# Causal attention on one core: value and output tables multiplied once, probabilities applied tile by tile, expert weights loaded behind the first key move

## The chip, the cores and the metric

One core of a Trainium2 chip runs a chain of eight layers (four attention-like, four feed-forward) on 4096 tokens of 128 features, all in one program. The metric is the device time of one launch in microseconds (us). Five engines run side by side, each in its own program order, and wait for each other by semaphores: TensorE (PE), VectorE (DVE), ScalarE (ACT), GpSimd (POOL) and SyncE (SP), which here issues the DMAs. PE's weight loads stand in a row of their own, PEld.

## The reference: what the touched stage computes

Only the third pair of layers is touched: causal attention with one head of 64 features, then a choice of one expert of eight per token. `x` is the residual stream, 8 chunks of 512 tokens; S and E of this layer are 512 and 128 here.

```python
q, k, v = x @ wq + bq, x @ wk + bk, x @ wv + bv          # 128 -> 64 each
w = softmax(q k^T / 8 + causal mask)                     # 512 x 512 per chunk
z = (w @ v) @ wo + bo                                    # 64 -> 128
# then, on the layer-normalised sum:
idx = argmax(xf @ Wg + bg)                               # one of 8 experts
h = gelu(xf @ W1[e] + b1[e])                             # all 8 are computed, 128 -> 128
y = h @ W2[e] + b2[e];  out = y[idx]
```

## The kernel before

`causal_and_gelu` (line 1815) builds the stage out of one instruction list per engine; nothing reorders them. A chunk c is 512 tokens, four tiles of 128. The loop `for s in steps` runs s from -2 to 8, and in one step the experts of chunk s stand between the second half of attention of chunk s+1 and the first half of chunk s+2. All matmuls are float32, which PE does in two passes (so the trace has two records for one matmul; a transpose is one).

One step on PE, in this order: `weigh(s+1)` (probabilities times values), `up(s, 0)` and `up(s, 1)` (two experts' first layer, each 512 tokens), `project(s+1)` (output table), `turn_first(s+2)` (transposes of the normalised tokens), `up` 2 and 3, `queries_and_keys(s+2)`, `values(s+2)`, `up` 4 to 7, `scores(s+2)`, then the four pieces of `down(s)` with `turn_second(s+1)`, `logits(s+1)`, `turn_prob(s+2)` and `turn_choice(s+1)` between them. `up(e)` waits for the gelu two before it, since there are two PSUM banks for it.

ACT in one step: `copy_weighed(s+1)` (z from PSUM to SBUF), gelu 0 and 1, `copy_first(s+2)`, gelu 2 and 3, `copy_queries_and_keys`, `copy_values`, gelu 4 to 7, `root(s+1)`, `exponentials(s+2)`, `copy_choice(s+1)`. A change of function table is an instruction of its own, ACT_TABLE_LOAD, placed ahead of the first operation that needs it: there are three in a step (gelu, square root, exponential).

DVE in one step: `add_output(s-1)` and its statistics, `keep_chosen(s, 1)` (expert 1's rows masked), `add_attention(s+1)` (scaled output added to x), `keep_chosen(s, 3)`, statistics, `normal_first(s+3)`, `keep_chosen` 5, 6, 7, `maxima(s+2)`, `normal_second(s+1)`, `copy_second`, `choose`, `copy_prob(s+2)`. POOL does `keep_chosen` 0, 2, 4 and `add_bias`.

SP issues, in order: the loads of the small tables, W1, b1, W2 and b2 of the experts (W1 and W2 are 512 KB each), and then per step `move_keys(st+2)` (the keys from partitions 64..127 of `qk` to `kT`, without which `scores` cannot start) and `spread_choice(st+1)` (the chosen rows to DRAM, and four loads that spread them over all partitions into `G`, which every `keep_chosen` needs).

The PSUM bank `ups` is shared in turn by the values, z, the projected output, the bias row, the logits and the choice. `bc` is the bias row (bv @ wo + bo); it waits for `copy_values(0)`.

Of the kernel before, what the change touches and what calls it, by code (L numbers as in the profile page):

```python
# [12 lines left out]
B, S, D = 8, 512, 128  # L13
# [1801 lines left out]
def causal_and_gelu(nc, net, d):  # L1815
# [8 lines left out]
    with ExitStack() as ctx:  # L1824
# [9 lines left out]
        xn1, xc, qk, kT, V = two("xn1", [TC, D]), two("xc", [S]), two("qk", [S]), two("kT", [S], H), two("V", [TC, H])  # L1834
        nb, sums, ri, prob = two("nb", [TC]), two("sums", [TC]), two("ri", [TC]), two("prob", [10 * P])
        PT, zT = [two(f"PT{k}", [(TC - k) * P]) for k in range(TC)], two("zT", [S], H)
# [19 lines left out]
        s_ready, nb_done, p_done, p_turned, PT_done, z_ready, z_done, o_ready = (  # L1856
            p.sem(n) for n in ("s_ready", "nb_done", "p_done", "p_turned", "PT_done", "z_ready", "z_done", "o_ready"))
# [23 lines left out]
        def _(sp):  # L1881
# [14 lines left out]

            sp.dma_start(wqk[:, 0:H], a("wq")).then_inc(qk_loaded, 16)
# [9 lines left out]
            sp.dma_start(W1[:, :, :], d["L2_ffn_W1"].rearrange("e d f -> d e f")).then_inc(e_loaded, 16)  # L1907
            sp.dma_start(b1[:, :], d["L2_ffn_b1"]).then_inc(e_loaded, 16)
            sp.dma_start(W2[:, :, :], d["L2_ffn_W2"].rearrange("e f d -> f e d")).then_inc(e_loaded, 16)
            sp.wait_ge(rest_zeroed, 1)  # L1910
            sp.dma_start(b2[0:E, :], d["L2_ffn_b2"]).then_inc(e_loaded, 16)
# [41 lines left out]
        def _(pe):  # L1953
# [36 lines left out]
            def weigh(c):  # L1990
                pe.wait_ge(PT_done, c + 1)
                pe.wait_ge(v_done, c + 1)
                wait_for(pe, ohT_done, c - 1)
                for k in range(TC):
                    last = nc.tensor.matmul(ups[0:H, k * P:S], V[c % 2][:, k, :], PT[k][c % 2][:, :],
                                            start=(k == 0), stop=(k == TC - 1))
                last.then_inc(z_ready, 1)

            def project(c):
                pe.wait_ge(z_done, c + 1)  # L2000
                for k in range(TC):
                    last = nc.tensor.matmul(ups[:, tok(k)], zT[c % 2][:, tok(k)], wo[:, :], start=True, stop=True)
# [42 lines left out]
            for s in steps:  # L2045
# [9 lines left out]
                if here(s + 1):  # L2055
                    project(s + 1)
# [16 lines left out]
                if here(s + 2) and s + 1 != 0:  # L2073
# [29 lines left out]
        def _(act):  # L2103
            def copy_weighed(c):
                act.wait_ge(z_ready, c + 1)
                wait_for(act, o_ready, c - 2)
                nc.scalar.activation(zT[c % 2][:, :], ups[0:H, :], ACT.Copy).then_inc(z_done, 1)
# [20 lines left out]
            def copy_values(c):  # L2128
                act.wait_ge(v_ready, c + 1)
                wait_for(act, z_ready, c - 2)  # L2130
                nc.scalar.activation(V[c % 2][:, :, :].rearrange("p a b -> p (a b)"), ups[:, 0:TC * H],
# [1034 lines left out]
```

## Time and profile before

| | us |
|---|---|
| median of 3 runs (lowest, highest) | 1577.16 (1574.89, 1578.33) |
| the profiled execution: its own time | 1576.58 |
| its span, first to last instruction | 1574.8 |
| the touched stage in that span | 1056.0 to 1331.7 |
| PE, DVE, ACT, POOL busy over the span | 1288.2, 1029.2, 802.3, 535.9 |
| granted TensorE clock over the span | 0.885 of full speed |

The touched stage is a sixth of the span. Two kinds of stretch stand in it: a start of some 60 us, in which the first two chunks go through attention with little beside them, and eight steps of about 28 us. Busy shares over the whole span say little about it; the places of the stage have to be read in the timeline.

### The profile page before, as it was taken

To read this page: it belongs to the slowest core of one execution; us is meant where nothing else is said; L and a number is where in the kernel's file an instruction comes from. 1 tells how busy PE (TensorE), PEld (TensorE's weight loads), DVE (VectorE), ACT (ScalarE), POOL (GpSimd) and SP (SyncE) were. 2 spreads that over 40 slices of the span, in tenths; PEclk is the share of its full clock that TensorE was granted. 3 is DMA by queue.
4 is the path that set the end of the run, shared out by engine and by line. 5 is a ranking of instruction groups with operands and counts; after the bars stand their busy time and mean duration, and the time that the engine had idled before them with its cause. 6 is when DMAs were issued, how large, how long until landed. Compare 5 with 4: busy or idle time off the path is not lost. (4 is left out here: it accounts for less than half of the span.)

```text
span 1574.8 us, 21830 instructions
## 1 busy us (share of the span) xinstructions
PE 1288.2 (82%) x6696; PEld 718.4 (46%) x6696; DVE 1029.2 (65%) x2781; ACT 802.3 (51%) x1606; POOL 535.9 (34%) x668
## 2 busy tenths in 40 slices
PE   5899999999997128935589989875899997689898
PEld 1223333333333118932345555643466755577633
DVE  7778888888853665635987785323467653566486
ACT  2467777776783004527646543312455452456554
POOL 3342343343210006358455345330112112333046
PEclk7799999999998558975699999985799998699999
DMA  5211111111105302210023333321132131000001
GB/s 151 57 49 30 52 48 41 42 52 52 32 12 157 70 1 66 59 36 24 8 55 70 72 76 55 76 39 34 58 112 62 62 107 57 30 2 1 1 21 34
DMA packets 80774, 81.15 MB, mean 52 GB/s; under 512 B 19899, under 2 KB 64139, under 8 KB 80659
## 3 DMA queue, kind: packets, MB, share of 16 engines
q1 hardware_dynamic: 77327, 74.06, 18.0%
q0 software_dynamic: 2304, 4.72, 1.3%
q8 instruction: 54, 0.88, 0.2%
q10 hardware_dynamic: 1028, 0.98, 0.2%
q14 instruction: 61, 0.50, 0.1%
HBM read 64.32 MB, written 13.92 MB: 50 GB/s over the span
## 5 line engine op out<-in xcount | busy, mean ns | idle before, releaser
L933 DVE TENSOR_REDUCE a_nm<-a_aps 128x1 f32<-128x512 f32 x512 | 333.5, 686 | 75.2 <-PE a_aps L698 75.2
L897 ACT ACTIVATE a_prob<-a_sps 128x512 f32<-128x512 f32 x512 | 271.4, 597 | 114.6 <-PE a_sps L710 113.6
L698 PE MATMUL a_aps<-a_K,a_Q 96*128 96x512 bf16 x512 | 195.1, 401 | 13.0 <-DMA a_K<-k_parts 12.7
L710 PE MATMUL a_sps<-a_Q,a_K 99*128 99x512 bf16 x512 | 156.2, 385 | 1.2 <-ACT a_prob L897 1.2
L1402 POOL TENSOR_TENSOR p_h<-p_sl,p_t 128x512 f32<-128x512 f32 x72 | 105.5, 1484 | 143.3 <-ACT p_sl L1542 74.3
L719 PE MATMUL a_ops<-a_prob,a_Vg 128*32 128x512 f32 x1024 | 136.9, 609 | 0.0
L698 PEld LDWEIGHTS a_aps<-a_K,a_Q 96*128 96x128 bf16 x512 | 50.3, 98 | 140.7 <-DVE a_nm L933 90.4
L1542 ACT ACTIVATE p_sl<-p_up_a 128x512 f32<-128x512 f32 x72 | 42.9, 597 | 112.5 <-PE p_up_b L1432 112.5
L1928 POOL TENSOR_TENSOR c_h<-c_h,c_G 128x512 f32<-128x512 f32 x24 | 31.7, 1325 | 181.0 <-ACT c_h L2114 163.8
L407 POOL CAST a_ms<-a_mr 16x128 bf16<-16x128 f32 x32 | 9.0, 280 | 243.0 <-ACT a_mr L855 243.0
L1432 PE MATMUL p_up_b<-x_normT,p1w_w 128*128 128x512 f32 x144 | 76.4, 613 | 7.9 <-DVE p_t L1650 7.6
L1650 DVE TENSOR_TENSOR p_t<-p_G,p_up_b 128x512 f32<-128x512 f32 x64 | 43.8, 685 | 53.5 <-PE p_up_b L1432 33.2
L710 PEld LDWEIGHTS a_sps<-a_Q,a_K 99*128 99x128 bf16 x512 | 49.8, 99 | 61.1 <-ACT a_prob L897 30.5
L1430 PE MATMUL p_up_a<-x_normT,p1w_w 128*128 128x512 f32 x144 | 74.8, 601 | 1.5 <-ACT p_sl L1542 1.5
L1440 PE MATMUL p_yps<-p1w_w,p_h 128*128 128x128 f32 x576 | 68.6, 282 | 3.2 <-POOL p_h L1402 3.2
L1440 PEld LDWEIGHTS p_yps<-p1w_w,p_h 128*128 128x128 f32 x576 | 67.9, 199 | 4.4 <-issue 3.2
L1204 ACT ACTIVATE m0e_hT<-m0e_hps,m0e_ws 128x128 f32<-128x128 f32 x160 | 45.6, 368 | 41.3 <-PE m0e_hps L1173 41.3
L2041 PE MATMUL c_yps<-c_W,c_h 128*128 128x128 f32 x512 | 64.0, 279 | 0.0
L2275 DVE TENSOR_TENSOR c_h<-c_h,c_G 128x512 f32<-128x512 f32 x40 | 39.9, 1017 | 35.8 <-ACT c_h L2114 32.5
L2031 PE MATMUL c_hps<-c_xT,c_W 128*128 128x512 f32 x128 | 61.9, 613 | 0.0
L2041 PEld LDWEIGHTS c_yps<-c_W,c_h 128*128 128x128 f32 x512 | 61.3, 196 | 0.0
L1155 POOL DMA_INDIRECT m0e_x<-tokens,m0w_token x40 | 39.7, 992 | 49.5 <-PE m0e_xps L1166 23.4
(571 smaller groups left out, 2702.2 us busy)
## 6 DMA issues: line engine op xcount, KB each, us to landing
p_G<-gates_by_expert SPq DMA_DIRECT2D x32, 512.0 KB, 6.9
c_G<-choice_rows SPq DMA_DIRECT2D x32, 512.0 KB, 6.4
a_Q<-q_parts SPq DMA_DIRECT2D x192, 32.0 KB
a_K<-k_parts SPq DMA_DIRECT2D x31, 96.0 KB
q_parts<-a_partsq SPq DMA_DIRECT2D x7, 384.0 KB, 2.8
k_parts<-a_partsk SPq DMA_DIRECT2D x7, 384.0 KB, 2.8
token_outputs<-m0e_y SPq DMA_DIRECT2D x40, 64.0 KB, 1.5
m0w_w<-in_L_ffn_W SPq DMA_DIRECT2D x1, 2048.0 KB, 9.4
```

The lines of the kernel that those rows point to most:

```text
L698: nc.tensor.matmul(aps[n % 3][:, :], Q[0:MAX, head, q * P:(q + 1) * P], K[0:MAX, head, :], start=True, stop=True).then_inc(a_ready, 1)
L710: nc.tensor.matmul(sps[(NS * u + k) % 3][:, :], K[0:KB, head, k % TC * P:(k % TC + 1) * P], Q[0:KB, head, :], start=True, stop=True).then_ ...
L719: last = nc.tensor.matmul(ops[32 * j:32 * j + 32, :], Vg[u % 2][:, k, j, :], prob[u % 2][:, j, k, :], start=(k == 0), stop=(k == TC - 1))
L897: nc.scalar.activation(prob[u % 2][:, k // TC, k % TC, :], sps[n % 3][:, :], ACT.Exp).then_inc(p_done, 1)
L933: nc.vector.tensor_reduce(nm[u % 2][:, s:s + 1], aps[n % 3][:, :], AX.X, ALU.max, negate=True).then_inc(a_used, 1)
L1204: nc.scalar.activation(hT[t % 2][:, f, :], hps[t % 2][:, f * P:(f + 1) * P], ACT.Relu, bias=ws[t % 3][:, B1 + f:B1 + f + 1]).then_inc(h_do ...
L1402: nc.gpsimd.tensor_tensor(h[c % 2][:, j, :], sl[u % 3][:, :], t[u % 3][:, :], ALU.mult).then_inc(h_done, 1)
L1430: nc.tensor.matmul(up_a[u % 2][:, :], w1[:, j, :], net.xT[:, c * S:(c + 1) * S], start=True, stop=True)
L1432: nc.tensor.matmul(up_b[u % 2][:, :], w3[:, j, :], net.xT[:, c * S:(c + 1) * S], start=True, stop=True).then_inc(up_done, 1)
L1440: last = nc.tensor.matmul(yps[:, k, :], h[c % 2][:, j, k * P:(k + 1) * P], w2[:, j, :], start=(j == 0), stop=(j == NW - 1))
L2031: nc.tensor.matmul(hps[u % 2][:, :], W1[:, e, :], xT[c % 2][:, :], start=True, stop=True).then_inc(up_done, 1)
L2041: last = nc.tensor.matmul(yps[:, k, :], h[c % 2][:, e, tok(k)], W2[:, e, :], start=False, stop=(e == E - 1))
```

## The change

Since (w @ v) @ wo equals w @ (v @ wo), and v without its bias is x @ wv, the changed kernel multiplies wv by wo once (`join_tables`: one transpose of wv, a copy, one matmul, a copy) and lets `values` produce 128 projected features per token. `weigh` then gives the output itself, in PSUM with tokens on partitions: ten matmuls of a 128 x 128 probability tile (stationary) by a 128 x 128 value tile. `project` and `copy_weighed` are gone; the copy of the values is twice as wide. On SP the experts' loads stand behind the first key move, and on PE `scores(0)` stands ahead of `values(0)`.

```diff
-        xn1, xc, qk, kT, V = ..., two("V", [TC, H])
+        wvT, wvo = p.sb("wvT", [H, P]), p.sb("wvo", [P, D])
+        xn1, xc, qk, kT, V = ..., two("V", [TC, D])
...
+            def load_experts():          # the five lines that stood ahead of the loop
+                sp.dma_start(W1[:, :, :], d["L2_ffn_W1"].rearrange("e d f -> d e f")).then_inc(e_loaded, 16)
...
             for st in steps:
                 if here(st + 2):
                     move_keys(st + 2)
+                if st == -2:
+                    load_experts()
...
+            def join_tables():
+                pe.wait_ge(v_loaded, 16)
+                nc.tensor.transpose(ups[0:H, 0:P], wv[:, :], net.ident[:, :]).then_inc(wv_turned, 1)
+                pe.wait_ge(o_loaded, 48)
+                pe.wait_ge(wvT_done, 1)
+                nc.tensor.matmul(ups[:, P:P + D], wvT[:, :], wo[:, :], start=True, stop=True).then_inc(wvo_ready, 1)
+
             def values(c):
                 wait_for(pe, o_added, c - 1)
+                if c == 0:
+                    pe.wait_ge(wvo_done, 1)
                 for k in range(TC):
-                    last = nc.tensor.matmul(ups[:, H * k:H * (k + 1)], xc[c % 2][:, tok(k)], wv[:, :], start=True, stop=True)
+                    last = nc.tensor.matmul(ups[:, tok(k)], xc[c % 2][:, tok(k)], wvo[:, :], start=True, stop=True)
...
                 wait_for(pe, ohT_done, c - 1)
-                for k in range(TC):
-                    last = nc.tensor.matmul(ups[0:H, k * P:S], V[c % 2][:, k, :], PT[k][c % 2][:, :],
-                                            start=(k == 0), stop=(k == TC - 1))
-                last.then_inc(z_ready, 1)
-
-            def project(c):
-                pe.wait_ge(z_done, c + 1)
-                for k in range(TC):
-                    last = nc.tensor.matmul(ups[:, tok(k)], zT[c % 2][:, tok(k)], wo[:, :], start=True, stop=True)
+                for q in range(TC):
+                    for k in range(q + 1):
+                        last = nc.tensor.matmul(ups[:, tok(q)], PT[k][c % 2][:, tok(q - k)], V[c % 2][:, k, :],
+                                                start=(k == 0), stop=(k == q))
                 last.then_inc(o_ready, 1)
...
-                if here(s + 1):
-                    project(s + 1)
...
                     queries_and_keys(s + 2)
+                    if s + 2 == 0:
+                        join_tables()
+                        scores(s + 2)
                     values(s + 2)
...
-            def copy_weighed(c): ...     # z to SBUF
+            def copy_joined():
+                act.wait_ge(wv_turned, 1)
+                nc.scalar.activation(wvT[:, :], ups[0:H, 0:P], ACT.Copy).then_inc(wvT_done, 1)
+                act.wait_ge(wvo_ready, 1)
+                nc.scalar.activation(wvo[:, :], ups[:, P:P + D], ACT.Copy).then_inc(wvo_done, 1)
...
-                nc.scalar.activation(V[c % 2][:, :, :].rearrange("p a b -> p (a b)"), ups[:, 0:TC * H],
-                                     ACT.Copy).then_inc(v_done, 1)
+                nc.scalar.activation(V[c % 2][:, :, :].rearrange("p a b -> p (a b)"), ups[:, :], ACT.Copy).then_inc(v_done, 1)
...
-                if here(s + 1):
-                    copy_weighed(s + 1)
```

The first place is PE at the start of the stage, chunk 0 (`c_ups`, `c_sps` are PSUM, `c_wvo` the joined table). Before:

```order
L1963 MATMUL c_tps<-c_xc,c_wqk 128x512
L1968 MATMUL c_ups<-c_wv,c_xc 128x64 x4
L1978 MATMUL c_sps<-c_kT,c_qk 128x256
L1978 MATMUL c_sps<-c_kT,c_qk 128x128
L1978 MATMUL c_sps<-c_kT,c_qk 128x384
L1978 MATMUL c_sps<-c_kT,c_qk 128x512
L2078 MATMUL c_ups<-c_wo,c_bvb 128x128
```

and in the changed kernel:

```order
L1969 MATMUL c_tps<-c_xc,c_wqk 128x512
L1973 MATMUL c_ups<-ident,c_wv 64x128
L1976 MATMUL c_ups<-c_wo,c_wvT 128x128
L1993 MATMUL c_sps<-c_kT,c_qk 128x256
L1993 MATMUL c_sps<-c_kT,c_qk 128x128
L1993 MATMUL c_sps<-c_kT,c_qk 128x384
L1993 MATMUL c_sps<-c_kT,c_qk 128x512
L1983 MATMUL c_ups<-c_wvo,c_xc 128x128 x4
L2088 MATMUL c_ups<-c_wo,c_bvb 128x128
```

Two matmuls of the join stand ahead of the scores, and the values have moved from ahead of the scores to behind them. The second place is PE at the start of a middle step. Before:

```order
L2041 MATMUL c_yps<-c_W,c_h 128x128 x8
L1995 MATMUL c_ups<-c_PT,c_V 64x512
L1995 MATMUL c_ups<-c_PT,c_V 64x384
L1995 MATMUL c_ups<-c_PT,c_V 64x256
L1995 MATMUL c_ups<-c_PT,c_V 64x128
L2031 MATMUL c_hps<-c_xT,c_W 128x512 x2
L2002 MATMUL c_ups<-c_wo,c_zT 128x128 x4
L1958 MATMUL c_tps<-ident,c_xn 128x128 x4
```

and now:

```order
L2051 MATMUL c_yps<-c_W,c_h 128x128 x8
L2011 MATMUL c_ups<-c_V,c_PT 128x128 x10
L2041 MATMUL c_hps<-c_xT,c_W 128x512 x2
L1964 MATMUL c_tps<-ident,c_xn 128x128 x4
L2041 MATMUL c_hps<-c_xT,c_W 128x512 x2
```

Ten narrow matmuls stand for four wide ones, and the four of `project` are gone from between `up` and `turn_first`; the row ahead is the end of `down(s-1)`. The third place is ACT at the same point. Before:

```order
L2156 ACTIVATE c_ohT<-c_ups 8x512
L2107 ACTIVATE c_zT<-c_ups 64x512
L2114 ACT_TABLE_LOAD
L2114 ACTIVATE c_h<-c_hps,c_b 128x512 x2
L2119 ACTIVATE c_xc<-c_tps 128x512
```

and now:

```order
L2166 ACTIVATE c_ohT<-c_ups 8x512
L2125 ACT_TABLE_LOAD
L2125 ACTIVATE c_h<-c_hps,c_b 128x512 x2
L2130 ACTIVATE c_xc<-c_tps 128x512
```

The table load for gelu follows the copy of the choice directly; the copy of z, which waited for `weigh`, no longer stands between.

## Rows read from the trace of the kernel before

**Rows 1.** The page's first line.
```profile
span 1574.8 us, 21830 instructions
```

**Rows 2.** Busy time by stretch: us, then each engine's busy us (instructions), PEclk, DMA, GB/s.
```profile
1083.00:1118.00 35.00, 23.40 (x72) 13.06 (x72) 11.06 (x41) 7.94 (x16) 1.26 (x1) 0.60 0.17 64
1174.00:1202.00 28.00, 26.77 (x154) 18.61 (x153) 18.02 (x57) 14.62 (x25) 6.65 (x4) 1.00 0.25 81
```

**Rows 3.** Timeline, stage start: start us, length, engine, line, operation [idle before <- releaser].
```profile
1063.01 2.28 SPq L1911 DMA_DIRECT2D c_b<-in_L_ffn_b  x1
1063.06 1.81 PE L1968 MATMUL c_ups<-c_wv,c_xc 128*128 128x64 f32 x8
...
1063.30 0.78 ACT L2125 ACTIVATE c_qk<-c_tps,c_qkb,c_qks 128x512 f32<-128x512 f32 x1 [2.23 <-PE c_tps L1963]
...
1065.30 1.28 ACT L2147 ACT_TABLE_LOAD   x1
1065.33 0.50 SPq L1885 DMA_DIRECT2D c_kT<-c_qk  x1
...
1069.76 4.60 PE L1978 MATMUL c_sps<-c_kT,c_qk 64*128 64x256 f32 x8 [4.90 <-DMA c_kT<-c_qk]
...
1076.50 0.47 ACT L2147 ACTIVATE c_prob<-c_sps,c_nb 128x256 f32<-128x256 f32 x1 [9.92 <-DVE c_nb L2211]
...
1082.92 4.50 PE L1995 MATMUL c_ups<-c_PT,c_V 128*64 128x512 f32 x8 [1.82 <-issue]
...
1087.45 0.59 ACT L2107 ACTIVATE c_zT<-c_ups 64x512 f32<-64x512 f32 x1 [8.81 <-PE c_ups L1995]
...
1089.18 0.66 PE L1958 MATMUL c_tps<-ident,c_xn 128*128 128x128 f32 x4
```

**Rows 4.** Key moves (line 1885, eight of them), issue to landing.
```profile
DMA to landing us min/median/max: 2.2/2.2/4.3
```

**Rows 5.** Timeline of one middle step, chunk 1's experts beside chunks 2 and 3.
```profile
1142.67 0.59 ACT L2156 ACTIVATE c_ohT<-c_ups 8x512 f32<-8x512 f32 x1 [6.29 <-PE c_ups L2022]
...
1144.58 2.37 PE L1995 MATMUL c_ups<-c_PT,c_V 128*64 128x512 f32 x8
...
1146.87 0.30 PEld L2031 LDWEIGHTS c_hps<-c_xT,c_W 128*128 128x128 f32 x2 [0.17 <-issue]
...
1147.59 1.28 ACT L2114 ACT_TABLE_LOAD   x1
...
1148.79 1.16 PE L2002 MATMUL c_ups<-c_wo,c_zT 64*128 64x128 f32 x8
1148.89 1.27 ACT L2114 ACTIVATE c_h<-c_hps,c_b 128x512 f32<-128x512 f32 x2
...
1150.18 1.28 DVE L2275 TENSOR_TENSOR c_h<-c_h,c_G 128x512 f32<-128x512 f32 x1 [3.45 <-ACT c_h L2114]
...
1152.81 1.00 PEld L1968 LDWEIGHTS c_ups<-c_wv,c_xc 128*128 128x128 f32 x8 [0.53 <-DVE x_resid L2231]
...
1153.01 1.00 DVE L2275 TENSOR_TENSOR c_h<-c_h,c_G 128x512 f32<-128x512 f32 x1 [0.26 <-ACT c_h L2114]
...
1153.98 0.38 ACT L2131 ACTIVATE c_V<-c_ups 128x256 f32<-128x256 f32 x1
...
1164.04 0.42 PEld L2009 LDWEIGHTS c_tps<-ident,c_xn 128*128 128x128 f32 x4 [1.74 <-DVE c_xn L2250]
...
1173.08 0.19 PEld L1995 LDWEIGHTS c_ups<-c_PT,c_V 128*64 128x64 f32 x2
```

**Rows 6.** Timeline, steps of chunks 5 and 6.
```profile
1273.38 0.30 DVE L2207 TENSOR_TENSOR c_sps<-c_sps,c_mask 128x128 f32<-128x128 f32 x1 [0.34 <-PE c_sps L1978]
...
1297.65 0.69 DVE L2275 TENSOR_TENSOR c_h<-c_h,c_G 128x512 f32<-128x512 f32 x1 [0.16 <-ACT c_h L2114]
```

**Rows 7.** Timeline, last step.
```profile
1308.87 1.74 SPq L1894 DMA_DIRECT2D c_G<-choice_rows  x4
...
1313.34 5.13 POOL L1928 TENSOR_TENSOR c_h<-c_h,c_G 128x512 f32<-128x512 f32 x3 [17.13 <-DMA c_G<-choice_rows]
...
1319.90 3.45 PEld L2041 LDWEIGHTS c_yps<-c_W,c_h 128*128 128x128 f32 x16
...
1323.54 1.87 PEld L2041 LDWEIGHTS c_yps<-c_W,c_h 128*128 128x128 f32 x16
```

More of the change, by code:

```diff
@@ L1831, in causal_and_gelu @@
         W1, W2, b1, b2 = p.sb("W1", [P, E, P]), p.sb("W2", [P, E, D]), p.sb("b1", [P, E]), p.sb("b2", [P, D])
+        wvT, wvo = p.sb("wvT", [H, P]), p.sb("wvo", [P, D])
         rows = nc.dram_tensor("choice_rows", (B, E, S), FP, kind="Internal").ap()
         std = p.sb("std", [P, NT])
-        xn1, xc, qk, kT, V = two("xn1", [TC, D]), two("xc", [S]), two("qk", [S]), two("kT", [S], H), two("V", [TC, H])
+        xn1, xc, qk, kT, V = two("xn1", [TC, D]), two("xc", [S]), two("qk", [S]), two("kT", [S], H), two("V", [TC, D])
         nb, sums, ri, prob = two("nb", [TC]), two("sums", [TC]), two("ri", [TC]), two("prob", [10 * P])
-        PT, zT = [two(f"PT{k}", [(TC - k) * P]) for k in range(TC)], two("zT", [S], H)
+        PT = [two(f"PT{k}", [(TC - k) * P]) for k in range(TC)]
         bst1, bst2, std1 = two("bst1", [TC, 6]), two("bst2", [TC, 6]), two("std1", [TC])
@@ L1855, in causal_and_gelu @@
                                "v_done"))
-        s_ready, nb_done, p_done, p_turned, PT_done, z_ready, z_done, o_ready = (
-            p.sem(n) for n in ("s_ready", "nb_done", "p_done", "p_turned", "PT_done", "z_ready", "z_done", "o_ready"))
+        s_ready, nb_done, p_done, p_turned, PT_done, o_ready = (
+            p.sem(n) for n in ("s_ready", "nb_done", "p_done", "p_turned", "PT_done", "o_ready"))
+        wv_turned, wvT_done, wvo_ready, wvo_done = (p.sem(n) for n in ("wv_turned", "wvT_done", "wvo_ready", "wvo_done"))
         x_biased, o_added, measured, std1_done, xn2_done, x2_turned, xT_done = (
@@ L1895, in spread_choice @@
                                  rows[c, 2 * i:2 * i + 2, :].unsqueeze(0).to_broadcast([P, 2, S])).then_inc(G_loaded[i], 16)
+            def load_experts():
+                sp.dma_start(W1[:, :, :], d["L2_ffn_W1"].rearrange("e d f -> d e f")).then_inc(e_loaded, 16)
+                sp.dma_start(b1[:, :], d["L2_ffn_b1"]).then_inc(e_loaded, 16)
+                sp.dma_start(W2[:, :, :], d["L2_ffn_W2"].rearrange("e f d -> f e d")).then_inc(e_loaded, 16)
+                sp.wait_ge(rest_zeroed, 1)
+                sp.dma_start(b2[0:E, :], d["L2_ffn_b2"]).then_inc(e_loaded, 16)
             sp.dma_start(wqk[:, 0:H], a("wq")).then_inc(qk_loaded, 16)
@@ L2072, in _ @@
                     up(s, 7)
-                if here(s + 2) and s + 1 != 0:
+                if here(s + 2) and s >= 0:
                     scores(s + 2)
@@ L2103, in _ @@
         def _(act):
[L2104 to L2107, printed above, removed]
+            def copy_joined():
[3 more added lines that the diff above has]
+                nc.scalar.activation(wvo[:, :], ups[:, P:P + D], ACT.Copy).then_inc(wvo_done, 1)
             def gelu(c, e):
@@ L2174, in _ @@
                     copy_queries_and_keys(s + 2)
+                    if s + 2 == 0:
+                        copy_joined()
                     copy_values(s + 2)
@@ L2216, in copy_prob @@
                 v.wait_ge(p_turned, c + 1)
-                wait_for(v, z_ready, c - 2)
+                wait_for(v, o_ready, c - 2)
                 for k in range(TC):
```

8 lines of the change are left out of this document (1 added, 7 removed).

## The prediction, made before the changed kernel was run

> **What bounds the kernel now.** I read the page's first line for the span, then the stretches of the touched stage with their granted clock, then its timeline engine by engine, asking at each place which wait ends last. The span is 1574.8 us [rows 1]. All instructions that change lie in one stage of some 276 us, so I sum inside it and take what follows as moved and not changed. The stage has two regimes [rows 2]: from 1083 to 1118 PE is busy 23.4 of 35 us at a granted clock of 0.60, in a chain where each engine waits for the one before; from 1174 to 1202 it is busy 26.8 of 28 us at 1.00.
>
> In the start, PE waits 4.90 us for the keys: the copy of queries and keys ends at 1064.08, but SP issues the key move only at 1065.33, behind the 2.28 us of the last expert load, and the move lands 4.3 us later, where the other seven take about 2.2 [rows 3, 4]. In a middle step (weigh begins at 1144.58, the next at 1173.08, a pitch of 28.5) PE looks like the bound, but it is not in the first two thirds. The load of the gelu table starts only behind the copy of z, at 1147.59, and the first two gelus run from 1148.89 to 1150.16; DVE, idle 3.45 us, starts its mask on their end at 1150.18. From there DVE hardly stops until `turn_second`, for which PE had waited 1.74 us on 1164.04 [rows 5]. From `turn_second` to the next `weigh`, 9.04 us, PE goes without a wait. So the step is: gelu 1 (ACT), then DVE, then PE. What ends gelu 1 or the DVE chain earlier shortens the step; what only takes work off PE in its first part does not.
>
> **The change part by part: the start.** (1) Key move ahead of the experts' loads: issued at about 1064.1, landing 2.2 later, at 1066.3, so scores at 1066.4 instead of 1069.76, 3.4 earlier. Behind it in SP's queue now stand four loads; the next user of that queue is chunk 1's key move, some 25 us later, and the experts' first use is after 1118, so I cost them nothing. If the loads disturb the move in flight as before (4.3), 2.1 of the 3.4 are gone. The join must be over by then: PE ends queries and keys near 1063.3, one transpose, a copy behind the query copy (1064.1 to 1064.4), one matmul of two passes and a copy end near 1065.9; the scores only queue behind the matmul, near 1065.5. The margin is 0.8.
>
> (2) `values(0)` used to run in the shadow of the key move (1063.06, 1.81 us); now it stands behind the 4.60 us of the scores: 1066.4 + 4.6 + 1.8 = 1072.8. Its copy is 512 wide, for which I take the 0.59 of the copy of z, 1073.5. Only then does ACT reach the exponential's table load, which used to be over at 1066.6: 1.28, so exponentials at 1074.85 instead of 1076.50. The row maxima would be there at 1076.47 - 3.4 = 1073.1. Of 3.4 us, 1.65 are left [rows 3]. The Trainium skill speaks against this part: "ScalarE: Activation LUTs", What ACT_TABLE_LOAD costs, puts a switch at 1283 ns and a drain of about 1380 ns. This trace agrees with the first figure and not with the second: the load at 1147.59 is over at 1148.87 and the gelu starts at 1148.89 [rows 5]. With the page's drain the start would give 1.4 less and the time would be near 1571.0; I go by the row.
>
> (3) `weigh(0)` then begins at 1081.3. Old: 4.50 us at the low clock. New: 20 passes of 128 columns with 128-wide weights; the nearest row is the same form at the low clock, 16 in 3.45 us, 0.216 each, and the values' own 1.81 for 8; so 4.3 to 4.5, no difference. (4) The copy of z (0.59) and the projection between 1087.4 and 1089.18 go: `turn_first(1)` at 1085.7 instead of 1089.18, 3.5 earlier in all. (5) Given back: those four transposes ran at the full clock (0.66 us), as the clock had risen just after weigh; now they follow at once and I give them 1.1 (+0.45), and the wide copy of chunk 1's values, ahead of the square root on ACT, costs 0.59 - 0.38 = 0.2 [rows 3, 5]. Start: 2.8 us saved. Bounds: 1.1, if the clock stays low also through chunk 1's queries and values (another 1.7 by their 2.0 and 1.8 at the low clock), to 4.0, if it rises inside the new weigh.
>
> **The step of chunk 0's experts: 0.** There the load of the gelu table carries the wait for `up(0)`, in the old program and in the new, so the missing copy frees nothing; -0.2 to 0.5.
>
> **The middle steps, chunks 1 to 4.** Weigh at full clock: 20 passes at 1.87/16 = 0.117 [rows 7] are 2.3 us, against 2.37 now; equal. ACT is free at 1142.67 + 0.59 = 1143.26 and loads the gelu table at once, until 1144.5, with nothing to wait for: 1.28 us hidden under weigh. Then gelu 0 and 1 are bound by PE only: `up` 0 and 1 end at 1146.88 + 1.98 = 1148.86, gelu 1 ends 0.65 later at 1149.5 instead of 1150.16, so DVE's first mask and `add_attention` are 0.65 earlier, and `values`, which waited for it (0.53 us idle), too. `project` (1.16) goes from PE: `up` 2 and 3 come 1.1 earlier, so gelu 3 no longer holds DVE's second mask (0.26 us idle at 1153.01). DVE's chain is then 0.65 + 0.26 = 0.9 earlier; I take 0.85 as the reading has gaps of 0.05. The wider copy of the values, +0.2 on ACT, ends before `up(4)` and is covered by 0.5 us of ACT's idle time ahead of gelu 4. All other consumers have slack: PE idles 1.7 us before `turn_second`. Removed from PE, project's remaining 0.25 us goes into that idle time. Four steps: 3.4 us. Bounds per step 0.3 (if the masks lose more to POOL, below) and 1.4 (if DVE loses less to it).
>
> **Chunk 5 and 6.** In chunk 5's step there is no `normal_first`, and the scores end last (DVE idle 0.34 on them), so only the 0.65 of `values` comes through: 0.6. In chunk 6's, DVE waits 0.16 for the last gelu; the gelus come over 1 us earlier, DVE's chain 0.65 + 0.16: 0.8 [rows 6]. Chunk 7 has no weigh: 0.
>
> **Sum.** 2.8 + 0 + 3.4 + 0.6 + 0.8 = 7.6 us. The profiled execution took 1576.58 us, 1.8 outside the span, and would become 1569.0; the median of the three runs is 0.58 above it, 1577.16, and I predict from that: **1569.6 us**.
>
> **The rivals.** *(A) More than that, 1567.* The new weigh is of the form that at 1319.90 ran 16 passes in 3.45 us and the next 16 in 1.87: the clock rose within some 3.5 us, where the old weigh of 64 columns took its whole 4.50 at half [rows 3, 7]. If it rises within the new weighs, chunk 0 saves 0.5 in weigh and the 0.45 on the transposes, chunk 1 0.5; with DVE losing less to POOL in two or three steps the sum is 10. Against: the rise is not tied to the form alone, as one row can't tell.
>
> *(B) Only the start counts, 1574.* The two masks need the spread rows `G`. In the last step, where they are wanted early, POOL gets the first at 1313.34, 4.5 us after SP issued (1308.87) [rows 7]. In a middle step the issue is just behind the start of weigh, so they land 4.6 after it. Gelu 0 would now end at 4.1 and gelu 1 at 4.9. POOL's mask thus waits 0.5, DVE's just not. If the rows land 0.7 later in these steps, DVE's mask is where it was, and of the step's gain 0.2 stays: 1577.2 - 2.8 - 0.9 = 1573.5, or 1574 with a poor start. For it: the margin is only 0.3, and POOL and DVE slow each other (1.28 us for a mask that takes 0.69 alone [rows 5, 6]). Against: the 4.5 holds for all four loads in flight.
>
> *(C) The change doesn't reach the path, within 0.2%.* The join is late or the key move still lands after 4.3, and the steps give nothing: 1577.2 - 0.7 = 1576.5.
>
> *(D) Slower, by the clock.* In the middle steps PE is busy 26.8 of 28 us at 1.00; at half clock each such microsecond costs one more. Ten short matmuls with a weight load each, after a start with shorter bursts, could leave the clock at half beyond weigh(1). For it: from 1083 to 1118 two thirds busy gave only 0.60 [rows 2]. It decides from 10.8 us of PE work newly at half clock (7.6 + 3.2); if the first step of experts stays at half, 1569.6 + 26 = 1596. Against: right behind weigh come matmuls of 512 columns, and the narrow passes at 1319.90 did raise it.
>
> **How the numbers follow.** Forecast 0.60, A 0.17, B 0.12, C 0.06, D 0.05. What can be told from no change here is about 0.2%, 3.2 us: below 1574.0 is faster. Forecast, A and over half of B lie there: 0.84; the rest of B and C are the same: 0.11; D 0.05. Range: the start's bounds are -1.7 and +1.2, the steps' -2.2 and +2.2; together, as both ends at once are unlikely, and reaching to A and to most of B, 1566.3 to 1573.5.
>
> **What would show it.** Right: the key move issued right behind the query copy and landing in about 2.2 us; scores some 3.4 us earlier from the stage's start; exponentials of chunk 0 only 1.65 earlier, with the table load directly ahead of them; in the middle steps the gelu table load standing right behind the copy of the choice, DVE's wait for the first gelus shorter by 0.65, a pitch of about 27.6 instead of 28.5, PE's idle time before `turn_second` nearly as now. Wrong: masks that wait for the `G` load (B), a granted clock below 1.00 after the first experts (D), a gap between the table load and the first exponential (the page's drain), or a weigh that is longer than 2.4 us at the full clock, which would be the loads of weights not hidden.

## The result, and the profile after

| | before | after |
|---|---|---|
| median (lowest, highest), four runs each | 1576.03 us (1570.42, 1578.33) | 1564.09 us (1563.39, 1564.24) |
| profiled execution: its own time | 1576.58 us | 1564.02 us |
| its span | 1574.8 us | 1562.3 us |

The ratio is 0.9924, with an interval of 0.9903 to 0.9944: 11.9 us faster. The forecast was 1569.6 us, a gain of 7.6; the direction was right, and the time lies 2.2 us below the low end of its range. Of the 5.5 us between, 1.1 is the base: the kernel before has a median of 1576.03 here and not the 1577.16 that I started from. Of the rest, in the profiled pair, 2.1 lie in the touched stage and 2.8 in stages that nobody touched; 0.6 goes off, as that pair differs by 12.56 us and the medians by 11.94.

I cut each trace at three places: the first load of the touched stage, the first weight load (row PEld) of each of its `weigh`s, and the first load of the stage that follows, whose code is the same in both kernels. All lengths below are differences of such starts; in the new form the first matmul of a `weigh` stands 0.11 us behind its weight load from weigh(2) on.

| us | before | after | gain |
|---|---|---|---|
| stages ahead (same code) | 1056.00 | 1057.83 | -1.83 |
| touched stage: start to weigh(1) | 57.59 | 56.32 | 1.27 |
| step of chunk 0's experts | 30.99 | 29.64 | 1.35 |
| chunks 1 to 4 | 28.50, 27.86, 28.50, 28.50 | 27.54, 27.27, 27.22, 27.67 | 3.66 |
| chunk 5 | 27.87 | 27.25 | 0.62 |
| weigh(7) to the end of the stage | 46.91 | 44.07 | 2.84 |
| last stage (same code) | 242.08 | 237.49 | 4.59 |

So the touched stage is 9.74 us shorter, where the sum said 7.6. The last stage, which nobody touched, gave 4.6 us more, and the stages ahead took 1.8 back. First the page's first line and the two stretches that answer to [rows 1, 2]:

```profile
span 1562.3 us, 21889 instructions
...
1087.00:1122.00 35.00, 23.05 (x92) 16.65 (x91) 11.53 (x42) 10.60 (x19) 2.27 (x2) 0.67 0.17 65
1170.00:1198.00 28.00, 26.14 (x165) 19.44 (x164) 18.57 (x58) 14.95 (x26) 5.54 (x4) 1.00 0.23 81
```

The middle steps run at the full clock as before; the start still spends its time mostly at half. The timeline of the start, the same places as [rows 3]:

```profile
1065.93 0.50 SPq L1887 DMA_DIRECT2D c_kT<-c_qk  x1
...
1066.48 0.59 SPq L1900 DMA_DIRECT2D c_W<-in_L_ffn_W  x1
...
1070.03 4.61 PE L1993 MATMUL c_sps<-c_kT,c_qk 64*128 64x256 f32 x8 [3.06 <-DMA c_kT<-c_qk]
...
1074.56 2.07 PE L1983 MATMUL c_ups<-c_wvo,c_xc 128*128 128x128 f32 x8
...
1077.29 1.28 ACT L2157 ACT_TABLE_LOAD   x1
...
1078.58 0.47 ACT L2157 ACTIVATE c_prob<-c_sps,c_nb 128x256 f32<-128x256 f32 x1
...
1085.00 4.60 PE L2011 MATMUL c_ups<-c_V,c_PT 128*128 128x128 f32 x20 [1.82 <-issue]
...
1089.40 0.75 PE L1964 MATMUL c_tps<-ident,c_xn 128*128 128x128 f32 x4
...
1114.15 3.84 PE L2011 MATMUL c_ups<-c_V,c_PT 128*128 128x128 f32 x20 [1.77 <-DVE c_PT L2230]
```

and the answer on the eight key moves, which stands for [rows 4]:

```profile
DMA to landing us min/median/max: 2.2/2.2/4.0
```

The key move is issued directly behind the query copy, as forecast. It did not land in 2.2 us: the scores start 4.1 us behind its issue, with the first expert load issued 0.55 us after it. Counted from the stage's start the scores are 1.6 us earlier (12.20 against 13.76), not 3.4, and the exponentials, behind the table load, 0.25 us later. The second weigh, 4.5 us before, took 3.84: the clock rose to full 2.8 us behind its start, where it had risen 5.0 us behind it before. The middle step of chunk 1's experts, against [rows 5]:

```profile
1142.09 0.59 ACT L2166 ACTIVATE c_ohT<-c_ups 8x512 f32<-8x512 f32 x1 [6.29 <-PE c_ups L2032]
...
1142.69 1.28 ACT L2125 ACT_TABLE_LOAD   x1
...
1143.90 2.40 PE L2011 MATMUL c_ups<-c_V,c_PT 128*128 128x128 f32 x20
...
1148.05 0.69 ACT L2125 ACTIVATE c_h<-c_hps,c_b 128x512 f32<-128x512 f32 x1 [0.17 <-PE c_hps L2041]
...
1148.53 1.26 POOL L1934 TENSOR_TENSOR c_h<-c_h,c_G 128x512 f32<-128x512 f32 x1 [18.62 <-DMA c_G<-choice_rows]
...
1148.77 1.57 DVE L2285 TENSOR_TENSOR c_h<-c_h,c_G 128x512 f32<-128x512 f32 x1 [2.63 <-ACT c_h L2125]
...
1151.55 0.68 DVE L2285 TENSOR_TENSOR c_h<-c_h,c_G 128x512 f32<-128x512 f32 x1
...
1162.49 0.42 PEld L2019 LDWEIGHTS c_tps<-ident,c_xn 128*128 128x128 f32 x4 [1.66 <-DVE c_xn L2260]
```

This is the step that the prediction drew: the table load stands right behind the copy of the choice, DVE waits 2.63 us for gelu 1 instead of 3.45, its second mask waits for nothing, and PE's idle time before `turn_second` is 1.66 us where it was 1.74. POOL's first mask does wait for the spread rows (the mechanism of rival B), but DVE's, at 1148.77, follows the end of gelu 1 at 1148.74. One term went another way than drawn: DVE's first mask took 1.57 us beside POOL's, 0.29 more than before, and its second 0.68 instead of 1.00. The end of the stage, against [rows 7]:

```profile
1313.61 1.53 PEld L2051 LDWEIGHTS c_yps<-c_W,c_h 128*128 128x128 f32 x13
```

The first sixteen weight loads of the last `down` took 3.45 us before; here the thirteen of them that the row shows stand in 1.53 us, 0.118 each, so the clock was already full. About 1.6 us of the tail's 2.84 is that.

The last stage in five executions, three of the changed kernel among them (columns: stretch, length, busy PE, PEld, DVE, ACT and POOL with counts, granted clock, DMA share, GB/s). First before and after:

```profile
1332.72:1574.80 242.08, 203.45 (x992) 132.94 (x992) 154.65 (x485) 132.37 (x339) 93.95 (x107) 0.90 0.05 15
```

```profile
1324.81:1562.30 237.49, 197.79 (x992) 129.51 (x992) 154.72 (x485) 132.28 (x339) 93.98 (x107) 0.93 0.06 15
```

then the changed kernel profiled a second and a third time:

```profile
1333.03:1575.00 241.97, 203.19 (x992) 132.83 (x992) 154.74 (x485) 132.50 (x339) 94.14 (x107) 0.90 0.05 15
```

```profile
1337.48:1574.10 236.62, 197.11 (x992) 129.18 (x992) 154.44 (x485) 132.50 (x339) 94.24 (x107) 0.94 0.05 15
```

and the kernel before with only its loads moved (experiment 3):

```profile
1342.30:1577.40 235.10, 195.56 (x992) 128.21 (x992) 154.39 (x485) 132.45 (x339) 94.35 (x107) 0.95 0.06 15
```

DVE, ACT and POOL do the same work in the same time each time; PE has the same 992 records and is busy 195.6 to 203.5 us. The length goes with the granted clock. Over all fourteen profiles of this study: 0.90 gives 242.0 and 242.1; 0.92 gives 239.1 to 239.6 (four); 0.93 gives 237.5 to 237.6 (four); 0.94 gives 236.4 to 236.6 (three); 0.95 gives 235.1. The changed kernel has 0.90, 0.93 and 0.94, the kernel before 0.90, 0.92 and 0.92. The ten profiles with the new form of the touched stage have last stages of 236.4 to 242.0 us, the four with the old form 235.1 to 242.1: no order with the code. Only one of the four runs of each kernel was profiled here, so how much of the 11.9 us of the medians is such chance can't be read from them; experiment 2 bears on it.

### The profile page after: what moved, and what is told of

Same layout as the page of the kernel before. It is cut to its first block and busy times, and to the rows that moved or that the text cites. A ratio compares the mean times of both kernels' runs of the same rounds, so it can differ in the third digit from the quotient of the medians.

```text
span 1562.3 us, 21889 instructions
## 1 busy us (share of the span) xinstructions
PE 1274.7 (82%) x6731; PEld 720.4 (46%) x6731; DVE 1028.1 (66%) x2781; ACT 799.4 (51%) x1600; POOL 534.6 (34%) x668
## 5 line engine op out<-in xcount | busy, mean ns | idle before, releaser
L1650 DVE TENSOR_TENSOR p_t<-p_G,p_up_b 128x512 f32<-128x512 f32 x64 | 43.7, 684 | 53.6 <-PE p_up_b L1432 33.1
L2125 ACT ACTIVATE c_h<-c_hps,c_b 128x512 f32<-128x512 f32 x64 | 43.9, 687 | 32.3 <-PE c_hps L2041 31.6
```

## The experiments

All ran on two other chips of the same kind, where the kernel before takes 1583 to 1586 us, so ratios to it are compared and not times. "Stage" is the touched stage, and the bracket behind a ratio is its 95% interval.

**1 and 2. Both kernels once more.** No edit: the two programs word for word, for a second profile and for the spread.

> The kernel before, unchanged, for its spread and a second profile. Of the 12.5 us by which the span fell, 9.7 lie in the touched stage and 4.7 in the last stage (242.1 before, 237.4 after), whose code is the same; the first stages were 1.8 longer. Theory P (chance of the clock): the length of the last stage changes by several us between executions of one program; then this profile's last stage is not the same 242.1, and the run times spread over 5 us or more. Theory F (fixed): the last stage is long because of how the old touched stage ends, and is 242 again, with run times within 2 us.

> The changed kernel, unchanged. Theory P: the four times within 0.9 us were chance, the last stage varies here too, and with more runs the difference of the medians comes nearer to the 9.7 of the touched stage. Theory F: last stage 237.4 again, times within 1 us, difference 12. Both: touched stage 267.0, weigh pitches 29.2, 29.6, then 27.2 to 27.7.

Measured: before again 1583.42 us over 12 runs (1577.48 to 1592.59) against 1582.84 over 33 (1578.28 to 1589.76), ratio 1.001 (0.9988 to 1.0031); stage 276.44, last stage 239.2. After again 1573.73, ratio 0.994 (0.9919 to 0.996); stage 267.28, last stage 242.0. So the stage's gain came again, 9.2, and the last stage's did not: it was 2.8 us longer with the changed kernel. Theory P of both texts held. With 10 runs against 33 the medians differ by 9.1 us, which is the stage's gain, and not by the 11.9 of four runs each. The rows of the changed kernel's second start:

```profile
1073.86 0.50 SPq L1887 DMA_DIRECT2D c_kT<-c_qk  x1
...
1076.29 4.60 PE L1993 MATMUL c_sps<-c_kT,c_qk 64*128 64x256 f32 x8 [1.39 <-DMA c_kT<-c_qk]
...
1084.84 0.47 ACT L2157 ACTIVATE c_prob<-c_sps,c_nb 128x256 f32<-128x256 f32 x1
...
1091.26 4.13 PE L2011 MATMUL c_ups<-c_V,c_PT 128*128 128x128 f32 x20 [1.82 <-issue]
...
1095.22 0.60 PE L1964 MATMUL c_tps<-ident,c_xn 128*128 128x128 f32 x4
```

The stage starts at 1065.75 here. The scores start 2.4 us behind the issue of the key move this time, 3.2 us earlier in the stage than before (forecast 3.4), the exponentials 1.4 (1.65), `turn_first(1)` 3.7 (3.5), and the clock rises within the first weigh, so that its transposes take 0.60 and not the 1.1 that I had charged.

**3. Only the loads moved.** The diff shows the first of the moved lines.

```diff
 # on the kernel before: the four expert loads go behind the first key move
-            sp.dma_start(W1[:, :, :], ...)
             for st in steps:
                 if here(st + 2):
                     move_keys(st + 2)
+                if st == -2:
+                    sp.dma_start(W1[:, :, :], ...)
```

> The kernel before with one part of the change alone: the experts' loads behind the first key move. After the change the move was issued right behind the query copy but landed 4.1 us later, not 2.2. Theory 1 (the loads behind the move slow it all the same): landing 4.1 again, scores 1.5 us earlier than before from the stage's start, and since values(0) is still in the shadow and the exponential's table is loaded early, the whole 1.5 reaches weigh(0); the stage is about 1.5 shorter. Theory 2 (the landing of 4.1 came from the joined tables' traffic or the PE order): landing 2.2, stage 3.4 shorter. Pitches of the steps as before, 28.5 and 27.9.

Measured: 1578.48 us, ratio 0.9966 (0.9949 to 0.9983), but stage 276.79: no gain in the stage of the profiled execution, so neither theory's stage came. The move landed after 2.3 us. The first weigh does come 3.2 us earlier (23.66 us into the stage, 26.89 before), and the next stretch gives it all back, 33.78 us to the second weigh instead of 30.7. The stretches from 30 to 50 us into the stage, before first:

```profile
1086.00:1096.00 10.00, 5.14 (x28) 3.38 (x26) 4.85 (x22) 3.93 (x6) 1.26 (x1) 0.84 0.06 13
1096.00:1106.00 10.00, 8.45 (x24) 5.09 (x24) 4.09 (x15) 0.66 (x2) 0.00 (x0) 0.50 0.00 0
```

and with only the loads moved:

```profile
1095.51:1105.51 10.00, 5.83 (x20) 3.98 (x20) 4.84 (x22) 3.34 (x5) 1.28 (x1) 0.50 0.06 13
1105.51:1115.51 10.00, 8.30 (x24) 4.93 (x24) 4.24 (x15) 0.81 (x2) 0.00 (x0) 0.50 0.00 0
```

Before, the clock was full from 31.9 to 38.7 us into the stage, the stretch of chunk 1's queries, keys and values (0.84 on average in the first row); now it is at half right through. `project`, `turn_first`, queries and keys, and values, before:

```profile
1088.10 1.16 PE L2002 MATMUL c_ups<-c_wo,c_zT 64*128 64x128 f32 x8 [0.68 <-ACT c_zT L2107]
1089.18 0.66 PE L1958 MATMUL c_tps<-ident,c_xn 128*128 128x128 f32 x4
1090.53 1.12 PE L1963 MATMUL c_tps<-c_xc,c_wqk 128*128 128x512 f32 x2 [0.69 <-ACT c_xc L2119]
1091.49 1.00 PE L1968 MATMUL c_ups<-c_wv,c_xc 128*128 128x64 f32 x8
```

and with only the loads moved:

```profile
1094.38 2.07 PE L2003 MATMUL c_ups<-c_wo,c_zT 64*128 64x128 f32 x8 [0.68 <-ACT c_zT L2108]
1096.38 1.11 PE L1959 MATMUL c_tps<-ident,c_xn 128*128 128x128 f32 x4
1098.18 2.07 PE L1964 MATMUL c_tps<-c_xc,c_wqk 128*128 128x512 f32 x2 [0.69 <-ACT c_xc L2120]
1100.05 1.81 PE L1969 MATMUL c_ups<-c_wv,c_xc 128*128 128x64 f32 x8
```

They take 3.1 us longer together, which is what was given back. What the profiled time gained lies in the last stage, 235.1 us. But the median of 12 runs gained 4.4 us, with an interval clear of nothing, and this one profile does not explain that: the clock's stretch may fall otherwise in other executions. How much the loads' move alone is worth stays open.

**4. Only the join.** The changed kernel with the loads back ahead of the first key move.

```diff
+            load_experts()
             for st in steps:
                 if here(st + 2):
                     move_keys(st + 2)
-                if st == -2:
-                    load_experts()
```

> The changed kernel with the experts' loads back at the head of SP's list. Both theories: steps as in the changed kernel (pitches 27.2 to 27.7). The start loses what the early move gave: scores 1.5 us later, weigh(0) at 28.7 from the stage's start against 27.1, the stage about 1.5 longer than the changed kernel's, 268.5, if nothing else in the start hides it.

Measured: 1576.95 us, ratio 0.9951 (0.9929 to 0.9972); stage 270.83 (268.5 was expected), 5.6 us shorter than the kernel before's. The start gives 0.3 of that (57.40 to weigh(1)), the steps and the tail the rest: chunks 1 to 4 27.29, 27.61, 27.44 and 27.84. So in the profiles the join is worth 5.6 us and the key move 3.5 more on top of it, 3.3 of them at the start; alone (experiment 3) it kept nothing. The 3.5 are more than the 1.5 expected, since the move landed after 2.3 us in experiment 2 and not after 4.0. The medians say it otherwise: 5.9 us for the join, 4.4 for the loads alone, 9.1 for both, so nearly a plain sum. Their intervals are some 3 us wide to each side and don't decide between the two.

**5. A dead copy where the copy of z stood.** On ACT, behind `weigh` and ahead of gelu 0, of the same size.

```diff
+            def dead_copy(c):
+                act.wait_ge(o_ready, c + 1)
+                nc.scalar.activation(dead[:, :], net.xT[0:H, 0:S], ACT.Copy)
...
             for s in steps:
+                if here(s + 1):
+                    dead_copy(s + 1)
```

> The changed kernel with a copy of 64 x 512 on ACT, from SBUF and used by nobody, where the copy of z stood: it waits for weigh, so the gelu table loads behind it again, while project stays gone from PE. The pitches of chunks 1 to 4 were 28.3 before and 27.4 now. Theory 1 (gelu 1's end is what starts DVE's chain): about 28.2, the 0.65 of gelu 1 is lost and only DVE's old wait of 0.26 for gelu 3 stays saved. Theory 2 (PE's 1.16 us of project were the gain): 27.4 as now.

Measured (one run): 1582.19 us, stage 272.49; chunks 1 to 4 28.05, 28.08, 28.04 and 28.07, where the second profile after has 27.27 to 27.60. In the trace:

```profile
1155.67 0.63 ACT L2122 ACTIVATE c_dead<-x_normT 64x512 f32<-64x512 f32 x1 [3.66 <-PE c_ups L2011]
1156.31 1.28 ACT L2129 ACT_TABLE_LOAD   x1
...
1158.90 1.29 DVE L2291 TENSOR_TENSOR c_h<-c_h,c_G 128x512 f32<-128x512 f32 x1 [3.41 <-ACT c_h L2129]
```

The table load is back behind a wait, and DVE waits 3.41 us for the gelus, as it did before (3.45). A copy of 0.63 us costs 0.6 us a step (28.06 against 27.47 on average), as it holds back the 1.28 us load. This is the larger part of what the middle steps had gained.

**6. A dead projection on PE.**

```diff
             def turn_first(c):
+                if c >= 1:
+                    for k in range(TC):
+                        nc.tensor.matmul(tps[:, tok(k)], wvT[:, :], wo[:, :], start=True, stop=True)
```

> The changed kernel with four matmuls of 128 columns on PE ahead of turn_first, where project stood, into a bank that turn_first overwrites; the gelu table still loads early. Theory 1 (the step needs both, gelu 1 for the first mask and gelu 3 for the second): gelu 3 ends as in the kernel before, so DVE waits for it at its second mask, and the pitch of chunks 1 to 4 is about 28.2. Theory 2 (ACT alone): 27.5. Theory 3 (PE alone): 28.5.

Measured (one run): 1573.29 us, stage 272.21; chunks 1 to 4 28.23, 27.61, 28.28 and 28.24.

```profile
1152.01 1.16 PE L1965 MATMUL c_tps<-c_wo,c_wvT 64*128 64x128 f32 x8
...
1154.65 0.69 ACT L2128 ACTIVATE c_h<-c_hps,c_b 128x512 f32<-128x512 f32 x1 [0.27 <-PE c_hps L2044]
...
1156.23 1.00 DVE L2288 TENSOR_TENSOR c_h<-c_h,c_G 128x512 f32<-128x512 f32 x1 [0.36 <-ACT c_h L2128]
```

With gelu 1 early and gelu 3 not, DVE's second mask waits again. Its start is 8.26 us behind the start of weigh in all four steps, whatever the first mask took (0.69 to 1.74 us): gelu 3 sets it. The average step is 28.09. Either 1.16 us on PE or 0.63 us on ACT takes 0.6 of the step's 0.9 us away: both halves of the change were needed. The prediction's shares, 0.65 and 0.26, are those of one order, the copy taken away first; without it alone, as here, only some 0.25 comes through.

**7. The loads only after the key move has landed.**

```diff
                 if st == -2:
+                    sp.wait_ge(k_moved, 16)
                     load_experts()
```

> The changed kernel, but SP waits until the first key move has landed before it issues the experts' loads. The move landed 4.0 us after its issue in one profile of the changed kernel and 2.3 in the other. Theory 1 (the loads that follow it sometimes overtake it in the DMA engines): 2.2 here, always, weigh(0) at 25.3 to 25.5 from the stage's start, median about 0.8 below the changed kernel. Theory 2 (the landing has its own spread): no difference to the changed kernel.

Measured: 1572.73 us, ratio 0.9929 (0.9906 to 0.9952), against 0.994 (0.9919 to 0.996) for the changed kernel on that chip: no difference can be told. The median expected, 0.8 us below the changed kernel, is too small a step for these intervals. The move lands after 2.2 us and the scores start there, with weigh(0) 25.4 us into the stage as theory 1 had it. With the loads right behind it, it took 4.0 in the first profile of the changed kernel and 2.3 in the five others with that order (experiments 2, 3, 5, 6 and 12). So the wait takes away at most a loss that came once in six; the one of 4.0 is also the only one from the first chip, and chance and chip can't be told apart.

**8 to 10. The clock of the start.** Unused matmuls of 512 columns, identity by an old tile into a PSUM bank that nobody needs yet, at seven places where PE waits in the start; nothing that is computed depends on them. The base is experiment 7.

```diff
+            def fill(n):
+                for _ in range(n):
+                    nc.tensor.matmul(hps[0][:, :], net.ident[:, :], net.xT[:, 0:S], start=True, stop=True)
```

Experiment 8 puts 4, 4, 4, 3, 8, 8 and 3 of them ahead of: the first `turn_first`, `scores(0)`, `turn_prob(0)`, `weigh(0)`, `turn_second(0)`, `turn_prob(1)`, `weigh(1)`. Experiment 9 puts 2, 2, 3, 2, 4, 5 and 2. Experiment 10 is 9 with a dead exponential of one column behind the join's copies:

```diff
                         copy_joined()
+                        nc.scalar.activation(dead[:, :], net.epst[:, 0:1], ACT.Exp)
                     copy_values(s + 2)
```

> As the one before, with matmuls of the identity by 512 columns of an unused tensor, into a bank that is free, in PE's waits of the start stretch (4, 4, 4, 3, 8, 8 and 3 of them): they only keep PE busy. In the start the granted clock is 0.50 but for 7 us behind weigh(0), in two profiles of the kernel before; with the loads moved alone it stayed 0.50 there too and the 3.2 us won at weigh(0) were gone by weigh(1). Theory 1 (what PE did before decides the clock): the clock is at 1.00 from chunk 0's scores on, scores, turns and weighs of both chunks take half, and weigh(2) comes 8 us or more earlier than 85; the stage about 259. Theory 2 (the filling costs what it gives): stage 267.

> The filled kernel with fewer unused matmuls: 2, 2, 3, 2, 4, 5 and 2 at its seven places instead of 4, 4, 4, 3, 8, 8 and 3 (each takes 0.88 us at full clock by the profile of the filled kernel). In that profile the fillers ended later than what they cover by some 2 us at the stage's start, 2 us ahead of the scores, 3.0 ahead of the second transposes of chunk 0, 2.6 ahead of chunk 1's probabilities and 0.6 to 0.7 at three more places, 11 us in all. Theory 1 (the start is a chain at half clock, and what keeps TensorE supplied keeps the clock at full): the granted clock stays at 1.00 through most of the start, two thirds of the 11 us come back, stage 256 us instead of 263.4, time near 1560 on a chip where the filled kernel takes 1567. Theory 2 (the fillers were only just enough, and fewer let the clock fall): stretches of the start at 0.5 to 0.7 again, scores of 4.6 us and a weigh of 4.5 us, stage 263 to 267, time 1567 to 1571.

> As the kernel with fewer fillers, and one exponential of one column into an unused tile stands behind the join's copies on ScalarE, so that the exponential's table is loaded while TensorE waits for the key move, and not behind the copy of chunk 0's values. Theory 1 (the start is a chain, and the table load of 1.28 us stands on it): the exponentials of chunk 0 come 1.3 us earlier, if the row maxima are there by then, and the stage is 1.0 to 1.3 us shorter than with fewer fillers alone. Theory 2 (the row maxima end no earlier than the load does): the exponentials wait for VectorE instead, gain below 0.3 us.

Measured, with the stage and its start up to weigh(1):

| | ratio (interval) | stage | start |
|---|---|---|---|
| 7 | 0.9929 (0.9906, 0.9952) | 267.57 | 54.14 |
| 8 | 0.9899 (0.9878, 0.992) | 263.41 | 52.34 |
| 9 | 0.9856 (0.9836, 0.9875) | 259.28 | 47.95 |
| 10 | 0.9873 (0.9849, 0.9898) | 255.88 | 47.05 |

In experiment 8 the clock stays full:

```profile
1071.69:1081.69 10.00, 9.22 (x31) 4.70 (x31) 3.07 (x9) 3.50 (x9) 1.92 (x2) 1.00 0.41 113
1081.69:1091.69 10.00, 9.31 (x53) 6.39 (x52) 4.25 (x18) 1.64 (x4) 0.58 (x1) 1.00 0.00 0
...
1086.50 2.39 PE L2016 MATMUL c_ups<-c_V,c_PT 128*128 128x128 f32 x20
...
1091.87 7.03 PE L1974 MATMUL c_hps<-x_normT,ident 128*128 128x512 f32 x16
1098.74 0.60 PE L2024 MATMUL c_tps<-ident,c_xn 128*128 128x128 f32 x4
```

The weigh takes 2.39 us instead of 4.13 to 4.6, but eight fillers take 7.03, and the transposes that stand behind them without a wait were held by them: I had counted too many, and the stage is 263.4 where I expected 259. With fewer, the start is 6.2 us shorter than in 7, 4.4 of which 8 had spent on fillers that came too late; the clock averages 0.86 over it. The stage was to be 256 and is 259.3. The fillers ahead of `turn_prob(1)` ran mostly at half clock and were late again, five of them in 6.50 us:

```profile
1105.10 6.50 PE L1974 MATMUL c_hps<-x_normT,ident 128*128 128x512 f32 x10
```

Experiment 9 also took the step of chunk 0 from 31.07 to 28.31, since weigh(1) and the matmuls behind it now ran at full clock. In experiment 10 the table load stands where PE waits for the keys:

```profile
1074.57 1.28 ACT L2202 ACT_TABLE_LOAD   x1
1075.86 0.20 ACT L2202 ACTIVATE c_dead<-eps_col 128x1 f32<-128x1 f32 x1
...
1082.32 0.47 ACT L2174 ACTIVATE c_prob<-c_sps,c_nb 128x256 f32<-128x256 f32 x1 [0.42 <-DVE c_nb L2239]
```

The exponentials start 1.4 us earlier in the stage than in 9 and wait for the row maxima now. But the scores stand 0.5 us earlier there too, so that no more than 0.9 is the early load's; the start is 0.9 us shorter. Of the 3.4 us by which the stage of 10 is shorter than that of 9, 2.9 are the tail, at a clock of 1.00 against 0.93. The medians of 9 and 10 can't be told apart. Both beat both kernels: 9 is 1.4% faster than the kernel before, the changed kernel 0.6 to 0.8%.

**11 and 12. A third profile of each.** No edit.

> The kernel before, word for word, for a third profile. The last stage (same code in both kernels) took 242.1 and 239.2 us in its two profiles, 237.5 and 242.0 in the two of the changed kernel. Theory P (the length of the unchanged last stage differs between executions by the clock that is granted in it, whatever ran before): somewhere between 235 and 242 us, in no order with the kernel. Theory Q (the change makes it shorter): 239 to 242 here and 236 to 238 in the changed kernel's third profile. By both the touched stage is 276.4 to 276.8 us.

> The changed kernel, word for word, for a third profile. Theory P: last stage 235 to 242 us, in no order with the kernel. Theory Q: 236 to 238 us, below that of the kernel before on the same chip. The touched stage is 267.0 to 267.6 us by both; if the key move lands after 4 us the first weigh stands at 27 us from the stage's start, if after 2.3 us at 25.4, and the stage is the same length only if the clock's rise inside the second weigh makes up for it.

Measured (one run each, same chip): before 1584.96 us, stage 276.84, last stage 239.1; after 1575.86, stage 269.08, last stage 236.6. By these two alone the last stage would seem shorter with the change, as theory Q has it; with the second pair (239.2 and 242.0) it does not, and the lengths go with the granted clock in all of them. The stage of the changed kernel was expected at 267.0 to 267.6 and is 1.5 us longer, at a tail with a lower clock. The stage's gain is 7.8 in this pair: start 3.7, chunk 0 0.15, chunks 1 to 4 3.05, chunk 5 0.6, tail 0.2 (clock 0.93 in it, 0.96 before).

## Why the prediction was wrong

The step that failed is the first: "I sum inside it and take what follows as moved and not changed". The code that follows is unchanged; its time is not. Without the 2.8 us that the untouched stages gave on balance, the time would have been 1566.9, inside the range. In the profiled pair the last stage gave 4.6 us, the stages ahead took 1.8, and in the tail of the touched stage a full clock gave some 1.6. Two profiles of one program differ by up to 5.4 us in the last stage alone (241.97 and 236.62 for the changed kernel), and 33 runs of the kernel before spread over 11.5 us, more than the 7.6 that I summed. My range came from terms inside the stage, 3.3 down and 3.9 up, and had nothing in it for this; three runs of before, 3.4 us apart, were in front of me, and the range should have had as much again at each end. That the miss came just in these four runs is bad luck: 9.1 us, the difference of the medians in experiment 2, would have fallen inside the range (1568.1 from the 1577.16 that I started from).

The Trainium skill, in "TensorE: Matmul & The Clock Gate", The HAM clock gate, says that what is lost until the clock rises varies from run to run and is under 1% of a typical kernel's span, and that one should not fit to a particular count of slow matmuls. The spread between runs is of that size here (11.5 of 1583 us is 0.7%), but so is the whole change, 0.6%, and so it decides whether a range holds. The loss itself was not measured over the kernel; experiment 9 wins 8.3 us of stage over 7, 0.5% of the span, mostly from the clock of this one start.

What is the change's own? The stage's gain is 9.7, 9.2 and 7.8 us in three pairs of profiles. By terms, as the mean of the three:

| | forecast | measured (three pairs) |
|---|---|---|
| start to weigh(1) | 2.8 | 2.8 (1.3, 3.6, 3.7) |
| chunk 0's step | 0 | 0.5 (1.35, 0, 0.15) |
| chunks 1 to 4 | 3.4 | 3.4 (3.7, 3.5, 3.05) |
| chunk 5 | 0.6 | 0.7 (0.6, 0.9, 0.6) |
| tail, with chunk 6's step | 0.8 | 1.4 (2.8, 1.2, 0.2) |
| sum | 7.6 | 8.9 (9.7, 9.2, 7.8) |

- *Start.* That the mean equals the forecast is luck: one execution fell 1.5 us short and two gave 0.8 and 0.9 more. I named the late landing of the key move (2.1 us) and gave it no weight in the sum; it came in one of the three profiles, where the scores were 1.6 us earlier instead of 3.4. Without it the start gives 3.6, since the 0.45 charged for transposes at half clock did not come: the clock rises within the new weigh, as rival A had it, in 4.13 us instead of 4.5. The values behind the scores took 2.07 us, not 1.8.
- *The table load in the start* cost its 1.28 us and no more: it ends at 1078.57 and the exponential starts at 1078.58, so the drain that the Trainium skill adds ("ScalarE: Activation LUTs", What ACT_TABLE_LOAD costs) is not seen here either.
- *Middle steps.* Right in mechanism and size, and shown by taking either half away (experiments 5 and 6). The DVE chain is not the sum of waits that I drew, though. Its first mask starts 0.73 us earlier behind weigh, and what it (1.22 to 1.73 us) and the second mask (0.68 to 1.41) then take, as they meet POOL's or not, makes most of the spread of the steps from 27.2 to 27.7.
- *Chunk 0 and the tail.* Where the clock rose early, chunk 0's step gave 1.35 (first profile), and the tail gave 2.8 at a clock of 1.00. At equal clock, 0.96, the tail is 46.6 to 46.9 in the old form (four profiles) and 45.2 to 45.8 in the new (four), 1.4 on average for a forecast of 0.8: this term was mis-sized. Where in the tail the other 0.6 lies was not looked into. In the new form the tail is 43.7 and 44.1 at a clock of 1.00, and 46.6 twice at 0.93.
- *Rivals.* A named a mechanism that exists (the clock inside the weighs) and came nearest, 1567; its worth in the stage was 1.7 us in the first profile (1.35 in chunk 0's step, the rest on the transposes) and 0.9 in the second (0.4 in the weigh, 0.5 on the transposes). B's wait exists on POOL and doesn't reach DVE. C and D did not occur in the join's steps; but the loss of the clock that D feared stands in experiment 3, at the other place: there an earlier weigh, of the old form, lost the full clock for the stretch behind it.

What stays open: why the stages ahead differ by up to 16 us in start from execution to execution and chip to chip (1056.0 to 1072.5 over all profiles, same code) was not looked into; nor is it shown why the clock rose 2.8 us behind the start of weigh(1) in the first profile of the changed kernel, and 4.6 to 5.8 us behind it in all the others without fillers, or why it did not rise behind weigh(0) in experiment 3.

## What to carry to other kernels

A copy that waits for TensorE, standing ahead of a change of function table on ScalarE, costs about its own time each step, since the load waits behind it (0.6 us in experiment 5); taking the copy away lets the load run under the matmuls. In a chain at half clock, count a moved transfer only with the clock that the moved work will meet, and put unused matmuls of counted length where TensorE waits (8.3 us of the stage in experiment 9). And a forecast for a kernel with dependent stretches at two clocks needs the spread of unchanged stages in its range, from several runs.

## What the runs showed of the hardware that was not expected

- The granted clock of an unchanged stage of 240 us varies between executions from 0.90 to 0.95, and its length with it from 242.1 to 235.1 us.
- A 128 KB move of keys took 2.2 us alone; with a 512 KB load issued 0.55 us behind it, 2.3 us in two executions of the changed kernel and 4.0 in one; behind such loads, 4.3 to 4.4 in all four profiles with that order.
- In one profile a transfer that let the first weigh start 3.2 us earlier was worth nothing: the chain behind it ran at half clock all through and gave back all but 0.2 us by the second weigh (experiment 3; its median of 12 runs gained 4.4 us all the same).
- DVE's mask takes 0.68 us alone and up to 1.74 beside POOL's (1.57 in the row above, 1.74 in experiment 6), longer than the 1.28 of [rows 5].
